# Edge counts from two columns beside the products, and another order of the low halves in two expert networks

## The chip, the cores and the metric

The kernel runs on one core of one Trainium2 chip. The metric is the device time of one execution in microseconds (us). All engines of the core work in parallel and wait for each other with semaphores: TensorE (PE; its weight loads are shown as PEld), VectorE (DVE), ScalarE (ACT), GpSimd (POOL) and the queue of SyncE (SP), which here only starts transfers.

## The reference, cut to what matters

Two graph blocks over 625 nodes of 768 numbers; each ends in a network of eight experts, of which every node takes two.

```python
def _rgcn_conv(x, src, dst, etype, W, root, b):         # twice in block 0
    seg = dst * num_rel + etype                         # 8 relations
    sums = segment_sum(x[src], seg)
    cnt = segment_sum(ones(edges), seg)
    mean = sums / maximum(cnt, 1.0)[:, None]
    out = einsum('nri,rio->no', mean, W)
    return out + x @ root + b

def _L0_ffn_ref(x, ...):            # 8 experts, three products each
    h = gelu(x @ W1[e] + b1[e])     # 768 -> 192
    h = gelu(h @ W2[e] + b2[e])     # 192 -> 384
    y = h @ W3[e] + b3[e]           # 384 -> 768
    out = out + comb[..., e:e+1] * y

def _L1_ffn_ref(x, ...):            # 8 experts, two products each
    h = gelu(x @ w1[e] + b1[e])     # 768 -> 1152
    y = h @ w2[e] + b2[e]           # 1152 -> 768
    out = out + y * gates[:, e:e+1]
```

## The kernel before, in words

Every fp32 matrix is split into a high half (the number rounded to fp32r, names in _hi) and a low half (what is left, names in _lo); a product is then three matmuls (`mm3`: lines 614, 617, 618), or two where one factor is exact. The 625 nodes are five tiles of 128 rows.

**Means of the first relational layer.** For each of the 8 relations r and each half c of 384 columns, the products of all nodes with W[r] are computed first, as rows ("products"). They go to HBM through `stage` and come back one half-relation h = 2r+c at a time (`back_load`, line 739) into one of three places (held0, product0, product1). ACT writes the high half (`part_back_hi`, line 1046), DVE the low half (`part_back_lo`, line 1594). The number of edges between each pair of nodes is an integer matrix `adj`; ACT turns the 5x5 blocks of relation r into `a_rel` (`convert`, line 1053). Then PE, in `means`, sums the products over the sources: for each of the five target tiles t ten matmuls (five source tiles, high and low; line 2395) into one of four banks in turn. At c = 0 five more matmuls with two columns of ones go first (line 2385); they give the edge count of each target row in another bank. DVE takes the count, limits it to 1 from below (line 1600), takes the reciprocal (line 1602), and adds sum times reciprocal to `acc_rows` (line 1618), which frees the bank: PE's tile number m waits until DVE is through with m-4 (`agg_used`). For h+1, DVE's low half stands ahead of the five additions of h.

**Experts.** The rows of the nodes are sorted into 17 slots of 128 rows, each with one expert. Network 0 (n = 0) has three layers, network 1 (n = 1) two. The work is a pipeline of turns: in one turn PE does layer 0 of slot v+1 (or v+2), then layer 1 (and 2) of the slots behind it. The weights of a layer come in units (n = 0: one unit for each layer, of 1152, 768 and 2304 columns; n = 1: three units of 2304 columns for each of the two layers). A unit is loaded by SP into one of four places `weight_raw` (line 780), split by ACT (`high`, line 1108) and DVE (`low`, line 1821) into one of four places of `weight_hi` and `weight_lo`, and used by PE. The load of unit u+4 waits for `low` of u, `high` of u+4 waits until PE has used u. ACT and DVE run four units ahead of PE.

The inputs of a layer are transposed by PE (line 2480): at the start of a turn the inner rows of layers 1 and 2 (`h_rows`, into `hT`), and, after the first unit of layer 0, the rows of the next slot (`slot_in`, into `xt`). ACT and DVE copy them out of the banks as high and low half (lines 1122 and 1831). The banks are few: in network 1 the transposes of `slot_in` use banks 5 and 6, which those of `h_rows` used before, so they wait for DVE's low half of `hT`. DVE copies the last layer's result out (`output`, line 1839); ACT sends it to HBM (`rows_out`, line 1135) and starts the load of a later slot (`rows_in`, line 1114).

Each engine works through its own list in the order in which the code writes it.

## Time and profile before

| | us |
|---|---|
| median of 3 runs | 2444.22 (2434.64 to 2444.30) |
| the profiled execution | 2444.68 |
| its span, first to last instruction | 2442.9 |
| PE busy | 2146.1 (88%) |
| PEld busy | 2054.8 (84%) |
| DVE busy | 1428.3 (58%) |
| ACT busy | 953.6 (39%) |
| POOL busy | 448.8 (18%) |
| means of the first relational layer | 605.2 to 775.0 |
| turns of the experts, n = 0 | about 1265 to 1425 |
| turns of the experts, n = 1 | about 2040 to 2416 |

Times of the profile count from the first instruction. Busy shares are means over stages with different limits. Matmuls are pipelined: one of 384 columns is shown as 0.34 us long and the next begins 0.17 us after it, so their starts tell the pace. A wait is written behind a row in brackets, with the engine and the line that ended it. An issue to the queues (SPq, ACTq) is not busy time.

### The profile page before, as it was taken

The numbers are of one execution on the slowest core, as the hardware profiler recorded it, in microseconds if no ns is written. First come the engines' busy times: TensorE is split into PE (matmuls) and PEld (weight loads), VectorE is DVE, ScalarE is ACT, GpSimd is POOL, SyncE is SP. The second block draws the span as 40 slices with busy tenths as digits, with TensorE's granted clock in tenths as the row PEclk, the third lists the DMA queues.
The fourth block names the chain that finished last, engine by engine and source line by source line (L and its number), as shares of the span: only waits on it lengthen the run. The fifth ranks groups of instructions, "written<-read, shape, count | busy, mean of one in ns | idle before, by whom it ended". The sixth has DMA issues, their size and how long they took to land. (4 is left out here: it accounts for less than half of the span.)

```text
span 2442.9 us, 32630 instructions
## 1 busy us (share of the span) xinstructions
PE 2146.1 (88%) x13045; PEld 2054.8 (84%) x13045; DVE 1428.3 (58%) x2288; ACT 953.6 (39%) x1249; POOL 448.8 (18%) x230
## 2 busy tenths in 40 slices
PE   4898999999999999999968859788878968999994
PEld 4787999998999999999848849677778947999994
DVE  8555455554654133333458774358874677888884
ACT  1333166665332021112126623125522225777672
POOL 4771300000300533443010022211120020000001
PEclk9898999999999999999969979899999978999997
DMA  3412233333322111110259951110122038999995
GB/s 102 137 34 86 72 102 119 111 116 118 116 98 72 58 59 40 41 57 20 62 172 306 313 204 59 46 44 27 61 62 82 1 145 296 347 349 347 358 335 181
DMA packets 158240, 326.96 MB, mean 134 GB/s; under 512 B 14120, under 2 KB 99336, under 8 KB 158090
## 3 DMA queue, kind: packets, MB, share of 16 engines
q1 hardware_dynamic: 133354, 265.68, 31.9%
q10 hardware_dynamic: 18976, 43.33, 4.9%
q0 software_dynamic: 5760, 15.86, 2.1%
q8 instruction: 104, 1.70, 0.3%
q14 instruction: 46, 0.38, 0.0%
HBM read 278.24 MB, written 46.51 MB: 133 GB/s over the span
## 5 line engine op out<-in xcount | busy, mean ns | idle before, releaser
L614 PE MATMUL banks<-weight_hi,xt_hi 128*128 128x384 f32 (+2 forms) x2208 | 740.1, 335 | 69.5 <-DVE xt_lo L1372 14.4
L617 PE MATMUL banks<-weight_lo,xt_hi 128*128 128x384 f32 (+2 forms) x2208 | 723.7, 328 | 0.0
L618 PE MATMUL banks<-weight_hi,xt_lo 128*128 128x384 f32 (+2 forms) x2208 | 723.5, 328 | 0.0
L614 PEld LDWEIGHTS banks<-weight_hi,xt_hi 128*128 128x128 f32 x2208 | 428.5, 194 | 81.9 <-issue 26.4
L617 PEld LDWEIGHTS banks<-weight_lo,xt_hi 128*128 128x128 f32 x2208 | 428.6, 194 | 0.5 <-issue 0.4
L618 PEld LDWEIGHTS banks<-weight_hi,xt_lo 128*128 128x128 f32 x2208 | 427.6, 194 | 0.0
L1821 DVE TENSOR_TENSOR weight_lo<-weight_raw,weight_hi 128x2304 fp32r<-128x2304 f32 (+2 forms) x153 | 342.6, 2243 | 88.8 <-ACT weight_hi L1108 88.7
L1108 ACT ACTIVATE weight_hi<-weight_raw 128x2304 fp32r<-128x2304 f32 (+2 forms) x153 | 287.1, 1880 | 75.7 <-PE banks L614 45.5
L814 POOL TENSOR_TENSOR weight_hi<-weight_raw,zero_col 128x2304 fp32r<-128x2304 f32 (+1 forms) x23 | 95.8, 4164 | 790.9 <-PE banks L614 376.7
L2395 PE MATMUL banks<-held_hi,a_rel 128*128 128x384 f32 x550 | 189.1, 344 | 0.3 <-DVE held_lo L1594 0.3
L2395 PE MATMUL banks<-held_lo,a_rel 128*128 128x384 f32 x550 | 187.6, 341 | 0.0
L614 PE MATMUL banks<-weight_hi,hT_hi 128*128 128x384 f32 (+1 forms) x442 | 151.6, 343 | 25.5 <-DVE hT_lo L1831 25.5
L1588 DVE TENSOR_TENSOR held_lo<-banks,held_hi 128x384 fp32r<-128x384 f32 x80 | 44.6, 557 | 209.3 <-ACT held_hi L1041 209.3
L617 PE MATMUL banks<-weight_lo,hT_hi 128*128 128x384 f32 (+1 forms) x442 | 150.2, 340 | 0.0
L618 PE MATMUL banks<-weight_hi,hT_lo 128*128 128x384 f32 (+1 forms) x442 | 149.9, 339 | 0.0
L1041 ACT ACTIVATE held_hi<-banks 128x384 fp32r<-128x384 f32 x80 | 39.2, 490 | 242.0 <-PE banks L618 242.0
L1576 DVE TENSOR_TENSOR adj<-adj,banks 128x640 f32 x80 | 65.4, 818 | 116.2 <-PE banks L2367 116.2
L911 POOL TENSOR_TENSOR weight_lo<-weight_raw,weight_hi 128x1536 fp32r<-128x1536 f32 (+2 forms) x16 | 70.0, 4373 | 320.1 <-ACT weight_hi L987 320.1
L1053 ACT ACTIVATE a_rel<-adj 128x640 fp32r<-128x640 uint16 x80 | 58.2, 743 | 174.7 <-PE banks L2395 174.7
L816 POOL TENSOR_TENSOR weight_lo<-weight_raw,weight_hi 128x2304 fp32r<-128x2304 f32 (+1 forms) x23 | 124.5, 5412 | 1.8
L614 PEld LDWEIGHTS banks<-weight_hi,hT_hi 128*128 128x128 f32 (+1 forms) x442 | 83.7, 189 | 29.6 <-DVE weight_lo L1821 21.7
L2395 PEld LDWEIGHTS banks<-held_hi,a_rel 128*128 128x128 f32 x550 | 105.3, 191 | 0.4 <-DVE held_lo L1594 0.4
(397 smaller groups left out, 3722.9 us busy)
## 6 DMA issues: line engine op xcount, KB each, us to landing
weight_raw<-L_ffn_w_in SPq DMA_DIRECT2D x102, 1152.0 KB, 6.4
weight_raw<-L_gnn_W_in SPq DMA_DIRECT2D x32, 1152.0 KB
weight_raw<-L_ffn_W_in SPq DMA_DIRECT2D x17, 1152.0 KB, 7.5
products<-bias_rows SPq DMA_DIRECT2D x80, 192.0 KB, 1.9
slot_in<-slot_rows ACTq DMA_DIRECT2D x34, 384.0 KB, 6.3
slot_out<-bias_rows ACTq DMA_DIRECT2D x34, 384.0 KB, 6.1
weight_raw<-L_ffn_W_in SPq DMA_DIRECT2D x17, 576.0 KB, 6.8
product_back<-products SPq DMA_DIRECT2D x10, 960.0 KB, 4.8
```

What stands on the lines that cost most here:

```text
L614: ins = pe.matmul(dst, s[0], m[0], start=start, stop=False)
L617: pe.matmul(dst, s[0], m[1], start=False, stop=False)
L618: return pe.matmul(dst, s[1], m[0], start=False, stop=stop)
L814: pool.tensor_tensor(hi, raw[s][0:rows, 0:n], zero_col[0:rows, :].broadcast_to([rows, n]), ALU.add).then_inc(hi_ready, 1)
L816: pool.tensor_tensor(lo, raw[s][0:rows, 0:n], f32(hi), ALU.subtract).then_inc(unit_ready, 1)
L911: pool.tensor_tensor(lo, raw[u.slot][:, 0:n], f32(hi), ALU.subtract).then_inc(unit_ready, 1)
L1053: act.activation(A_r[:, t, :, :], adj[:, r * TILES:(r + 1) * TILES, t * P:(t + 1) * P], ACT.Copy).then_inc(a_ready, 1)
L1108: act.activation(W4[u % RING][0][0:rows, 0:k * cols], RAW4[u % RAWS][0:rows, 0:k * cols], ACT.Copy).then_inc(e_hi[n], 1)
L1576: vec.tensor_tensor(block_of, block_of, ps[:, 2 * (s % 2):2 * (s % 2) + 2, 0:HALF], ALU.add).then_inc(slot_done, 1)
L1588: vec.tensor_tensor(lo[:, t, :], ps[:, part_bank(1, n), 0:WCOL], f32(hi[:, t, :]), ALU.subtract).then_inc(part_lo, 1)
L1821: vec.tensor_tensor(lo, RAW4[u % RAWS][0:rows, 0:k * cols], f32(hi), ALU.subtract).then_inc(e_lo[n], 1)
L2395: ins = pe.matmul(ps[:, agg_bank(m), 0:WCOL], A_r[:, t, src, :], part[:, src, :], start=(src == 0 and i == 0), stop=(src == FULL and i == 1))
```

## The change

1. **Counts.** The five matmuls with two columns of ones are gone, and with them the semaphore `cnt_full` and PE's wait for `cnt_ready`. The high halves of the three places have 386 columns instead of 384; ACT writes ones into the last two once for each place (`part_back_hi`, h < 3). At c = 0 the matmul with the high half is 386 columns wide, so that the count stands in column 384 of the same bank as the sums. For the last source tile the low half goes first, so that the wide matmul ends the bank. DVE takes the count from there, once all ten matmuls are done. In the second relational layer held0 keeps the row step of 386.
2. **Experts, DVE.** In each turn the low halves of `hT` and the output of the turn before go ahead of the last `low` of the turn before.
3. **Experts, n = 1.** The transposes of the next slot, their high and low halves and `rows_in` come after the second unit of layer 0 (`NEXT_AFTER`) and no longer after the first.
4. **Experts, ACT.** `rows_out` goes behind layer 0's part of the turn.
5. Small tensors are put together to make room for the 128 bytes `product_end`; the other tensors move by 64 or 128 bytes.

```diff
+OCOL = WCOL + 2
@@ places: the high halves of held0, product0 and product1 are [P, TILES, OCOL]
+        NEXT_AFTER = [0, 1]
@@ part_back_hi (ACT)
                 act.wait_ge(part_in[h % BACKS], 16 * (h // BACKS + 1))
-                act.activation(places[0][h % BACKS][0][:, :, :], back_rows[h % BACKS][:, :, :], ACT.Copy).then_inc(part_hi, 1)
+                hi = places[0][h % BACKS][0]
+                if h < BACKS:
+                    act.activation(hi[:, :, WCOL:OCOL], f32(ones_r[:, 0:TILES * (OCOL - WCOL)]).rearrange("p (t n) -> p t n", t=TILES), ACT.Copy)
+                act.activation(hi[:, :, 0:WCOL], back_rows[h % BACKS][:, :, :], ACT.Copy).then_inc(part_hi, 1)
@@ experts (ACT)
-                    if turn > 0:
-                        rows_out(turn - 1)
-                    for l, v in visits(n, turn):
+                    for i, (l, v) in enumerate(visits(n, turn)):
                         for j in range(parts(n, l)):
...
-                            if l == 0 and j == 0 and v + 1 < XSLOTS:
+                            if l == 0 and j == NEXT_AFTER[n] and v + 1 < XSLOTS:
                                 transposed_hi(0, v + 1)
                                 rows_in(v + 3)
                             high()
+                        if i == 0 and turn > 0:
+                            rows_out(turn - 1)
@@ inverse (DVE)
-                vec.wait_ge(cnt_full, r * TILES + t + 1)
-                order.step(vec.tensor_scalar(cnt_m[:, one], ps[:, (r * TILES + t) % 4, 0:1], 1.0, None, ALU.max))
+                m = agg_number(0, r, 0, t)
+                vec.wait_ge(agg_full, m + 1)
+                order.step(vec.tensor_scalar(cnt_m[:, one], ps[:, agg_bank(m), WCOL:WCOL + 1], 1.0, None, ALU.max))
@@ experts (DVE)
                         if l > 0:
                             transposed_lo(l, v)
+                    if turn > 0:
+                        output(turn - 1)
+                    if turn > turns(n)[0]:
+                        low()
+                    lows_left = sum(parts(n, l) for l, _ in visits(n, turn)) - 1
                     for l, v in visits(n, turn):
                         for j in range(parts(n, l)):
-                            if l == last and j == parts(n, l) - 1:
-                                output(v)
-                            if l == 0 and j == 0 and v + 1 < XSLOTS:
+                            if l == 0 and j == NEXT_AFTER[n] and v + 1 < XSLOTS:
                                 transposed_lo(0, v + 1)
-                            low()
+                            if lows_left > 0:
+                                low()
+                                lows_left -= 1
+                output(XSLOTS - 1)
@@ means (PE)
-                        if layer == 0 and c == 0:
-                            q = r * TILES + t
-                            if q >= 4:
-                                pe.wait_ge(cnt_ready, q - 3)
-                            for src in range(TILES):
-                                ins = pe.matmul(ps[:, q % 4, 0:2], A_r[:, t, src, :], ones_r[:, 0:2], start=(src == 0), stop=(src == FULL))
-                            ins.then_inc(cnt_full, 1)
...
+                        wide_cols = OCOL if layer == 0 and c == 0 else WCOL
                         for src in range(TILES):
-                            for i, part in enumerate(places[layer][(2 * r + c) % len(places[layer])]):
+                            for part, cols in ((hi, wide_cols), (lo, WCOL)) if src < FULL else ((lo, WCOL), (hi, wide_cols)):
@@ layer, in the experts (PE)
-                        if l == 0 and j == 0 and v + 1 < XSLOTS:
+                        if l == 0 and j == NEXT_AFTER[n] and v + 1 < XSLOTS:
                             transposes_of(0, v + 1)
```

DVE in a turn of the second experts before, from the fifth `low` of a turn on (rows with x5 are five instructions):

```order
L1821 TENSOR_TENSOR weight_lo<-weight_raw,weight_hi 128x2304 x5
L1839 COPY bias_rows<-banks 128x384 x2
L1821 TENSOR_TENSOR weight_lo<-weight_raw,weight_hi 128x2304
L1831 TENSOR_TENSOR hT_lo<-banks,hT_hi 128x384 x3
L1831 TENSOR_TENSOR xt_lo<-banks,xt_hi 128x3x128 x2
```

And after the change, the same stretch:

```order
L1829 TENSOR_TENSOR weight_lo<-weight_raw,weight_hi 128x2304 x4
L1839 TENSOR_TENSOR hT_lo<-banks,hT_hi 128x384 x3
L1847 COPY bias_rows<-banks 128x384 x2
L1829 TENSOR_TENSOR weight_lo<-weight_raw,weight_hi 128x2304 x2
L1839 TENSOR_TENSOR xt_lo<-banks,xt_hi 128x3x128 x2
```

The three instructions on `hT` moved ahead of the two copies and of one split of weights; those on `xt` have two splits ahead of them and four behind.

DVE in a turn of the first experts before:

```order
L1821 TENSOR_TENSOR weight_lo<-weight_raw,weight_hi 128x2304
L1839 COPY bias_rows<-banks 128x384 x2
L1821 TENSOR_TENSOR weight_lo<-weight_raw,weight_hi 128x1152
L1831 TENSOR_TENSOR hT_lo<-banks,hT_hi 96x256
L1831 TENSOR_TENSOR hT_lo<-banks,hT_hi 128x384
L1831 TENSOR_TENSOR xt_lo<-banks,xt_hi 128x3x128 x2
L1821 TENSOR_TENSOR weight_lo<-weight_raw,weight_hi 96x768
```

And after:

```order
L1829 TENSOR_TENSOR weight_lo<-weight_raw,weight_hi 128x2304
L1839 TENSOR_TENSOR hT_lo<-banks,hT_hi 96x256
L1839 TENSOR_TENSOR hT_lo<-banks,hT_hi 128x384
L1847 COPY bias_rows<-banks 128x384 x2
L1829 TENSOR_TENSOR weight_lo<-weight_raw,weight_hi 128x1152
L1839 TENSOR_TENSOR xt_lo<-banks,xt_hi 128x3x128 x2
L1829 TENSOR_TENSOR weight_lo<-weight_raw,weight_hi 96x768
```

Here too `hT` goes ahead of the copies and of the unit of 1152 columns.

PE in the means, the end of one target tile at c = 0 and the start of the next, before:

```order
L2395 MATMUL banks<-product_hi,a_rel 128x384
L2395 MATMUL banks<-product_lo,a_rel 128x384
L2385 MATMUL banks<-ones_r,a_rel 128x2 x5
L2395 MATMUL banks<-product_hi,a_rel 128x384
L2395 MATMUL banks<-product_lo,a_rel 128x384
```

And after:

```order
L2405 MATMUL banks<-product_hi,a_rel 128x386
L2405 MATMUL banks<-product_lo,a_rel 128x384 x2
L2405 MATMUL banks<-product_hi,a_rel 128x386 x2
L2405 MATMUL banks<-product_lo,a_rel 128x384
L2405 MATMUL banks<-product_hi,a_rel 128x386
```

The five short matmuls are gone, and the order of high and low is turned round at the last source tile.

## Rows read from the trace of the kernel before

**Rows 1.** The page: busy tenths of PE and of DMA in 40 slices.

```profile
PE   4898999999999999999968859788878968999994
DMA  3412233333322111110259951110122038999995
```

**Rows 2.** Windows: from:to, length, busy (xcount) of PE, PEld, DVE, ACT, POOL; clock; DMA share, GB/s.

```profile
633.77:774.82 141.05, 141.05 (x876) 140.91 (x875) 78.19 (x153) 45.66 (x44) 0.00 (x0) 1.00 0.29 101
605.20:619.00 13.80, 13.48 (x49) 13.42 (x49) 3.89 (x2) 6.01 (x6) 9.99 (x3) 0.51 0.80 306
```

**Rows 3.** Timeline of PEld in the means: start, length, instruction, count, idle before.

```profile
642.77 0.70 PEld L2385 LDWEIGHTS banks<-ones_r,a_rel 128*128 128x128 f32 x5
...
643.50 0.19 PEld L2395 LDWEIGHTS banks<-product_lo,a_rel 128*128 128x128 f32 x1
643.68 0.19 PEld L2395 LDWEIGHTS banks<-product_hi,a_rel 128*128 128x128 f32 x1
```

**Rows 4.** All instructions of line 2385: count, duration min/median/max in ns.

```profile
L2385 PE MATMUL banks<-ones_r,a_rel x200: 165/250/352, 605.2 to 764.2; 128*128 128x2 f32 x100
```

**Rows 5.** Timeline of PE and DVE in the first relation.

```profile
606.72 0.69 PE L2395 MATMUL banks<-held_hi,a_rel 128*128 128x384 f32 x1 [0.28 <-DVE held_lo L1594]
...
616.57 3.61 DVE L1594 TENSOR_TENSOR product_lo<-product_back,product_hi 128x1920 fp32r<-128x1920 f32 x1 [9.91 <-ACT product_hi L1046]
...
621.46 0.42 PE L2395 MATMUL banks<-held_hi,a_rel 128*128 128x384 f32 x1
...
631.92 0.45 PE L2395 MATMUL banks<-product_hi,a_rel 128*128 128x384 f32 x1 [1.53 <-DVE acc_rows L1618]
```

**Rows 6.** Timeline of DVE at the start of a later relation.

```profile
656.64 2.16 DVE L1594 TENSOR_TENSOR product_lo<-product_back,product_hi 128x1920 fp32r<-128x1920 f32 x1 [1.79 <-ACT product_hi L1046]
658.71 0.15 DVE L1600 TENSOR_SCALAR cnt_m<-banks 128x1 f32<-128x1 f32 x1
...
659.10 0.62 DVE L1618 SCALAR_TENSOR_TENSOR acc_rows<-banks,inv,acc_rows 128x384 f32<-128x384 f32 x1
```

**Rows 7.** Who waited for whom in 2030 to 2443: total, times, longest.

```profile
PE banks L2480 <- DVE hT_lo L1831: 17.1, 14, 1.3
```

**Rows 8.** Timeline of PE, DVE and ACT in two turns of the second experts.

```profile
2205.13 0.92 PE L2480 MATMUL banks<-ident,slot_in 128*128 128x128 f32 x6 [1.19 <-DVE hT_lo L1831]
...
2221.62 1.14 PE L2480 MATMUL banks<-ident,h_rows 128*128 128x128 f32 x9
...
2223.57 1.01 DVE L1839 COPY bias_rows<-banks 128x384 f32<-128x384 f32 x2
...
2226.97 1.48 DVE L1831 TENSOR_TENSOR hT_lo<-banks,hT_hi 128x384 fp32r<-128x384 f32 x3
...
2224.02 0.85 ACT L1122 ACTIVATE hT_hi<-banks 128x384 fp32r<-128x384 f32 x2
...
2238.23 2.14 ACT L1108 ACTIVATE weight_hi<-weight_raw 128x2304 fp32r<-128x2304 f32 x1 [0.85 <-PE banks L614]
```

**Rows 9.** Windows of the experts: one turn and 15 us (n = 1); 15 us and 13 turns (n = 0).

```profile
2201.14:2223.57 22.43, 21.24 (x128) 20.82 (x127) 18.50 (x13) 15.86 (x15) 0.00 (x0) 1.00 0.96 347
2105.00:2120.00 15.00, 13.81 (x85) 13.39 (x84) 12.27 (x12) 9.33 (x10) 0.00 (x0) 1.00 1.01 380
1345.00:1360.00 15.00, 13.81 (x103) 13.48 (x101) 11.50 (x14) 10.14 (x14) 0.00 (x0) 1.00 1.02 315
1285.87:1405.00 119.13, 102.73 (x718) 99.16 (x716) 95.69 (x119) 79.49 (x118) 0.00 (x0) 1.00 0.97 310
```

**Rows 10.** DMA issues of the page: count, KB each, median us to landing (n = 1, n = 0).

```profile
weight_raw<-L_ffn_w_in SPq DMA_DIRECT2D x102, 1152.0 KB, 6.4
weight_raw<-L_ffn_W_in SPq DMA_DIRECT2D x17, 1152.0 KB, 7.5
```

**Rows 11.** Who waited for whom in 1275 to 1410 (n = 0).

```profile
PE banks L614 <- DVE hT_lo L1831: 18.3, 15, 1.7
ACT weight_hi L1108 <- DMA weight_raw<-L_ffn_W_in: 6.8, 4, 2.4
```

More of the change, by code:

```diff
@@ L38 @@
 WCOL = 384
+OCOL = WCOL + 2
+PRODUCT_END = 32
 UNIT = KD * WCOL
@@ L158, in build @@
             one, pair = allocator(here)
-            back_pairs = [pair(f"product{k}", [P, TILES, WCOL]) for k in range(2)]
+            back_pairs = [(one(f"product{k}_hi", [P, TILES, OCOL], F32R), one(f"product{k}_lo", [P, TILES, WCOL], F32R)) for k in range(2)]
         with ExitStack() as here:
@@ L254, in build @@
             one, _ = allocator(here)
-            one("held0_hi_place", [P, TILES, WCOL], F32)
+            one("held0_hi_place", [P, TILES, OCOL], F32)
             back_rows.insert(0, one("held0_back", [P, TILES, WCOL], F32))
-        held = [rg2("held0", [P, TILES, WCOL])]
+        held = [(rg("held0_hi", [P, TILES, OCOL], F32R), rg("held0_lo", [P, TILES, WCOL], F32R))]
         with ExitStack() as here:
@@ L2392, in means @@
                             pe.wait_ge(agg_used, m - 3)
+                        hi, lo = places[layer][(2 * r + c) % len(places[layer])]
+                        wide_cols = OCOL if layer == 0 and c == 0 else WCOL
                         for src in range(TILES):
-                            for i, part in enumerate(places[layer][(2 * r + c) % len(places[layer])]):
-                                ins = pe.matmul(ps[:, agg_bank(m), 0:WCOL], A_r[:, t, src, :], part[:, src, :],
-                                                start=(src == 0 and i == 0), stop=(src == FULL and i == 1))
-                                if unit_done and c == 0 and t == 0 and src == 0 and i == 0:
+                            for part, cols in ((hi, wide_cols), (lo, WCOL)) if src < FULL else ((lo, WCOL), (hi, wide_cols)):
+                                begin, end = src == 0 and part is hi, src == FULL and part is hi
+                                ins = pe.matmul(ps[:, agg_bank(m), 0:cols], A_r[:, t, src, :], part[:, src, 0:cols], start=begin, stop=end)
+                                if unit_done and c == 0 and t == 0 and begin:
                                     ins.then_inc(unit_used, 1)
```

24 lines of the change are left out of this document (11 added, 13 removed).

## The prediction, made blind

> **What bounds the kernel now.** I read the busy tenths of the page first: PE is near full almost everywhere, and DMA is near full in two places, the turns of the first experts (slices 21 to 23) and of the second (slices 34 to 39) [rows 1]. A change on PE's list outside these two counts in full; inside them it counts only as far as the transfers can follow. Then I read the stages that the diff touches. In the means PE has no gap from 633.77 on: 141.05 us busy in 141.05 us, at the full clock (1.00, 2.4 GHz), DMA at 0.29, DVE busy 78.19 [rows 2]. PE alone is the bound there. In a turn of the second experts PE works 21.24 of 22.43 us [rows 9] and the rest is one gap of 1.19 us, the transposes of `slot_in` waiting for `hT_lo` [rows 8]; it comes 14 times, 17.1 us [rows 7]. In the first experts PE works 102.73 of 119.13 us in 13 turns, 7.90 of 9.16 us for each [rows 9]; there the first matmul of layer 1 waits for the same kind of instruction, 15 times, 18.3 us in all [rows 11].
>
> **Counts.** Five short matmuls make the next tile late. Weight loads of matmuls with 384 columns start 0.174 us apart. With a group of five from 642.77 on, the second load behind it starts at 643.50 and the next at 643.68 [rows 3]; without the group they would be the second and third load from 642.77, at 642.94 and 643.12. So one group costs 0.56 us. There are 200 such matmuls, 40 groups [rows 4], 35 of them after 633.77. A sum that proves the price: seven relations are 700 matmuls of 0.1735, 121.5 us, and 35 groups of 0.56, 19.6 us; together 141.1 against the 141.05 measured [rows 2]. All 35 groups are on the path, since PE never waits there: 19.6 us.
>
> The other five groups are in the first relation, and I count nothing for them. PE starts it at 606.72, when the low half of held0 is there [rows 5], at half the clock (0.51, 1.2 GHz, until 619.00; PE had stood 2.4 us before) [rows 2], and ACT's new instruction, 10 columns wide, goes ahead of it and may cost 0.2. The fifth tile begins at 621.46 now. It needs the first bank, which DVE can't free before its low half of product0 is done, at 616.57 + 3.61 = 620.18, plus count, reciprocal and addition, about 1.0: 621.2. So the tile starts at most 0.3 earlier. Then DVE's next low half, slow beside POOL, holds PE until 631.92 (1.53 us) [rows 5]; PE that comes earlier only waits longer.
>
> The wide matmul streams 386 columns instead of 384. By the pace of 0.174 us for 384 that is 0.9 ns more, 200 times, 0.2 us. No row shows a row step of 386 or this width. The other end: two columns by themselves take 0.56/5 = 0.11 us, 22 us in all, which would eat the gain. Below nothing I exclude, since no column is saved. I take 0.2, as the columns follow one another in one stream, and keep the other end as a rival.
>
> DVE now takes the count after the ten matmuls. From the count to the addition are 0.39 us (658.71 to 659.10) and the addition takes 0.62 [rows 6]. That is 1.0 us for a tile, and PE needs the bank three tiles (5.2 us) later, so it is hidden, except where DVE comes late anyway: at the start of a relation the low half of the next product stands ahead. The relation of rows 6 starts on PE at 653.97, DVE frees its first bank at 659.72, 5.75 us later; PE's fifth tile will start after 4 x 1.735 = 6.94 us. A margin of 1.2 us is left, of 4.0 before. The list of ACT and the loads from HBM follow the same matmuls and move with them.
>
> **Second experts.** Set the start of a turn, 2221.62, to 0. Now DVE does two copies (from 1.95) and one `low` (2.5 us) and only then `hT_lo`, 5.35 to 6.8 [rows 8]. After the change `hT_lo` comes first. It waits for ACT's `hT_hi`, whose first part is there at about 2.9, and ends at about 4.5, 2.3 us earlier. The transposes that waited for it also move behind the second unit, to about 7.8. Both together leave over 3 us of margin; the gap goes. What is next on PE is its own work, 21.24 us for a turn.
>
> The postponed `low` ends 2.5 us later, and the load behind it starts later. It lands 6.4 us after its issue [rows 10]: 2226.97 + 2.5 + 6.4 = 2235.9. ACT needs it at 2238.23, or 1.2 earlier in a shorter turn, 2237.0 [rows 8]. So 1.1 us is left of what was 4.9. PE needs the unit some 4 us after ACT and DVE have split it, which covers a small delay.
>
> The limit is what all transfers can do. A turn of 22.43 us has a DMA share of 0.96, 21.5 us of full use, 347 GB/s. The best 15 us show a share of 1.01 and 380 GB/s [rows 9]. So a turn can't be shorter than 21.5/1.01 = 21.3 us, by chance PE's own 21.24. I take 1.0 us of the 1.19, as both are then full and no delay is made good: 14 turns, 14 us. The ends are 0 (transfers already give all) and 17.1.
>
> The Trainium skill, page "DMA: Bandwidth & Descriptors", section "Where 436 GB/s comes from", says that for transfers between HBM and SBUF about 358 GB/s of HBM is the limit. The 380 GB/s over 15 us speak against it on this core. By the rule a turn would take 347 x 22.43 / 358 = 21.7 us and the gain of this part would be 10 us instead of 14.
>
> **First experts.** Here `hT_lo` goes ahead of two copies (1.0 us) and a `low` of 1152 columns, and the gap of 1.2 us would go. But 13 turns have a share of 0.97 (8.9 us of 9.16), and the best 15 us have 1.02, at 315 GB/s [rows 9]: a turn can't be shorter than 8.9/1.02 = 8.7 us. ACT already waits for loads four times, 6.8 us [rows 11], and a large unit lands only after 7.5 us [rows 10]. I take 0.4 us for each of 15 turns, 6 us; the ends are 0 and 18.3. `rows_out` now stands behind layer 0; its buffer is written again two turns later, so it costs nothing, and ACT is free earlier for `h_rows`.
>
> **What it costs.** In the last turn of each network there is no layer 0 to cover the copies of slot 15: DVE does them after `hT_lo` now and PE waits for the first of the two, 0.5 us, twice: 1 us. `rows_in` and the three extra instructions of ACT are off the path.
>
> **The sum.** 2444.68 - 19.6 + 0.2 - 14 - 6 + 1 = 2406.3; the profiled execution was within 0.5 us of the median, 2444.22. One of the three runs was 10 us faster, which I can't explain. Forecast: 2406 us, its own range 2399 to 2413.
>
> **The rivals.**
> A, transfers are full in both experts: the gaps only change their name, from `hT_lo` to the loads. For it: shares of 0.96 and 0.97, and the waits for loads. Against it: 380 GB/s over 15 us. Then the counts gain 19.4 and the experts 3: 2444.7 - 22 = 2422. The page's limit of 358 GB/s is a weak form of it (2410, inside my own range). Chance 0.17.
> B, transfers hinder nowhere: both gaps go whole, 17.1 + 18.3 + 19.4 - 1 = 54: 2391. Against it speaks the best share in the first experts. Chance 0.12.
> C, DVE's chain in the means is late: the margin of 1.2 us is too small, say by 2 us in each of seven relations, 14 us: 2420. For it: the low half waits for ACT at each relation's start. Chance 0.07.
> D, 386 columns don't stream at the old pace: the gain of the counts is lost, 2425. Chance 0.04.
> E, slower: the postponed `low` starves the loads. They would have to land over 3 us later than the 6.4 and 7.5 us now, since ring and split cover that much. To lose the 19.4 us of the counts, all of some 30 turns must become 0.65 us longer than today. With 1.3 us for each: 2444.7 - 19.4 + 39 = 2464. Chance 0.02.
> The forecast has 0.55; 0.03 is left for mixtures.
>
> **Range and chances.** 2396 to 2423 takes in the forecast, A and C and a part of the mixtures, 0.8. A measurement of this kernel can tell about 0.5% (12 us) from no change. Faster by more: the forecast, A, B, C and most of D, 0.94; within 0.5%: 0.04; slower: 0.02.
>
> **What would show it.** In the means no row with two columns, PE full, and the stretch of seven relations 121.7 us long instead of 141.05. The fifth tile of each relation must not wait for the addition (C), and the matmuls with 386 columns must start 0.174 us apart (D). In the second experts: no wait of the transposes for `hT_lo`, the copies of line 1847 about 21.4 us apart, DMA share near 1. In the first: 8.7 us apart. Waits of ACT's `weight_hi` for loads instead would mean A, turns of 7.9 us B. I would be wrong most easily in the size of what the transfers allow.

## The result, and the profile after

The changed kernel takes **2411.47 us** (median of 4 runs, 2405.89 to 2420.97), the kernel before 2443.45 us beside it: a ratio of **0.9886, 95% interval 0.9862 to 0.9910**, some 28 us (22 to 34) less. The forecast was 2406 us, 2396 to 2423.

The busy tenths of PE and DMA on the page after, which answer to [rows 1]. No slice differs from before by more than one tenth: at this grain the page doesn't show the change.

```profile
PE   4898999999899999999969849788888868999994
DMA  3412223332432111110159951110122027999995
```

Windows of after (from:to, length, busy and count of PE, PEld, DVE, ACT, POOL; clock; DMA share, GB/s): 135 us of the means, 12 turns of the second experts, 14 turns of the first. They answer to [rows 2, 9].

```profile
629.00:764.00 135.00, 135.00 (x758) 134.82 (x757) 88.81 (x166) 48.63 (x48) 6.99 (x2) 0.98 0.32 113
2103.01:2359.54 256.53, 255.22 (x1520) 252.21 (x1519) 219.83 (x157) 187.95 (x169) 0.00 (x0) 1.00 0.97 365
1276.87:1398.90 122.03, 107.62 (x747) 104.17 (x746) 103.94 (x126) 85.90 (x123) 0.00 (x0) 1.00 0.91 309
```

PE has no gap in the means, and none to speak of in the second experts (21.38 us for a turn, was 22.43). In the first experts a turn takes 8.72 us (was 9.16), and PE still idles 14.4 us of 122. Who waits there now (total us, times, longest), from 1265 to 1410 us, and ACT alone in the second experts, from 1968 to 2391 us:

```profile
ACT weight_hi L1115 <- DMA weight_raw<-L_ffn_W_in: 28.0, 26, 2.4
...
PE banks L618 <- DVE hT_lo L1839: 14.3, 10, 4.4
PEld banks L618 <- DVE weight_lo L1829: 13.2, 8, 4.7
```

```profile
ACT weight_hi L1115 <- DMA weight_raw<-L_ffn_w_in: 74.0, 48, 4.3
```

Before, ACT waited 6.8 us for loads in the first experts [rows 11], and in the second the list of its waits from 2030 us on has none for a load. The 17.1 us of [rows 7] are gone.

Next I cut both profiles at the same matmuls. These are windows of before and, below them, of after: the relations' products, the means, layer 2, the first experts, the part between, the second experts.

```profile
309.27:606.72 297.45, 294.74 (x1749) 273.05 (x1748) 150.00 (x324) 194.45 (x251) 0.00 (x0) 1.00 0.34 111
606.72:776.23 169.51, 166.75 (x995) 166.11 (x996) 95.85 (x177) 53.11 (x52) 20.23 (x4) 0.96 0.32 112
776.23:1211.79 435.56, 426.06 (x2450) 425.22 (x2451) 141.25 (x209) 72.49 (x132) 158.28 (x45) 0.99 0.13 41
1211.79:1442.23 230.44, 169.59 (x1039) 153.97 (x1040) 163.84 (x268) 118.40 (x172) 22.96 (x19) 0.86 0.79 259
1442.23:1917.89 475.66, 388.96 (x2597) 371.50 (x2598) 298.83 (x663) 146.49 (x261) 70.92 (x17) 0.92 0.17 57
1917.89:2415.10 497.21, 444.07 (x2582) 426.25 (x2580) 387.38 (x416) 284.78 (x269) 13.89 (x23) 0.94 0.75 277
```

```profile
314.44:613.66 299.22, 295.12 (x1743) 273.33 (x1743) 150.11 (x324) 194.77 (x252) 0.00 (x0) 1.00 0.33 110
613.66:765.37 151.71, 144.84 (x800) 144.22 (x800) 95.72 (x177) 53.24 (x54) 20.18 (x4) 0.97 0.35 125
765.37:1204.64 439.27, 429.77 (x2450) 428.92 (x2451) 141.34 (x209) 72.70 (x132) 158.36 (x45) 1.00 0.13 41
1204.64:1428.88 224.24, 168.48 (x1039) 153.74 (x1040) 164.57 (x268) 119.23 (x172) 22.95 (x19) 0.86 0.78 265
1428.88:1908.41 479.53, 395.75 (x2597) 378.30 (x2598) 298.88 (x663) 146.66 (x261) 72.06 (x18) 0.90 0.17 56
1908.41:2391.53 483.12, 443.99 (x2582) 428.88 (x2580) 383.36 (x416) 281.05 (x269) 13.89 (x23) 0.94 0.76 285
```

The three stages that the diff touches give 17.8 + 6.2 + 14.1 = 38.1 us, almost what I had summed (38.4, with 1 us for the ends taken off). But the spans differ by only 23.7 us. 5 us are start-up: the first matmuls with `rf` start at 34.3 to 34.9 us in some executions and at 39.6 to 40.2 in others, whatever the kernel. The rest stands in rows that nobody looks at after such a change: **layer 2 has the same 2450 matmuls and the same 9.5 us in which PE is idle, and takes 3.7 us more**; the relations' products take 1.8 more, the part between 3.9. That was the open question.

One thing ahead: executions of one kernel differ by up to 20 us here (before: 2425 to 2451 over all runs). The profiles show where: 5 us at the start, and up to 12 us between 104 and 241 us, in the first mixer (124.8 to 137.2 us, whatever the kernel). No part of the change is there. I didn't look for its cause. So I compare stages of profiles for what is under 10 us, and ratios of many runs for the rest.

### The profile page after: what moved, and what is told of

It reads as the page before. It is cut to its first block and busy times, and to the rows that moved or that the text cites. A ratio compares the mean times of both kernels' runs of the same rounds, so it can differ in the third digit from the quotient of the medians.

```text
span 2419.2 us, 32227 instructions
## 1 busy us (share of the span) xinstructions
PE 2134.1 (88%) x12845; PEld 2045.4 (85%) x12845; DVE 1429.5 (59%) x2288; ACT 951.5 (39%) x1252; POOL 450.8 (19%) x230
## 5 line engine op out<-in xcount | busy, mean ns | idle before, releaser
L818 POOL TENSOR_TENSOR weight_hi<-weight_raw,columns 128x2304 fp32r<-128x2304 f32 (+1 forms) x23 | 95.7, 4160 | 784.0 <-PE banks L618 360.9
L2405 PE MATMUL banks<-held_hi,a_rel 128*128 128x384 f32 (+1 forms) x550 | 172.5, 342 | 9.7 <-DVE acc_rows L1626 5.6
L2405 PE MATMUL banks<-held_lo,a_rel 128*128 128x384 f32 x550 | 169.3, 340 | 0.0
L621 PE MATMUL banks<-weight_lo,hT_hi 128*128 128x384 f32 (+1 forms) x442 | 151.2, 342 | 0.0
L622 PE MATMUL banks<-weight_hi,hT_lo 128*128 128x384 f32 (+1 forms) x442 | 150.9, 341 | 0.0
```

Of the source, the lines that this page charges most:

```text
L621: pe.matmul(dst, s[0], m[1], start=False, stop=False)
L622: return pe.matmul(dst, s[1], m[0], start=False, stop=stop)
L818: pool.tensor_tensor(hi, raw[s][0:rows, 0:n], zero_col[0:rows, :].broadcast_to([rows, n]), ALU.add).then_inc(hi_ready, 1)
L2405: ins = pe.matmul(ps[:, agg_bank(m), 0:cols], A_r[:, t, src, :], part[:, src, 0:cols], start=begin, stop=end)
```

## Experiments

**1. Each part by itself, and the two halves of the experts' part.** `counts_only` has the counts' part alone, `experts_only` the experts' part alone. `move_only` and `order_only` are counts_only with one more edit each. move_only moves the transposes of `slot_in`:

```
         NEXT_AFTER = [0, 1]
...
-                            if l == 0 and j == 0 and v + 1 < XSLOTS:
+                            if l == 0 and j == NEXT_AFTER[n] and v + 1 < XSLOTS:
```

order_only is the changed kernel with `NEXT_AFTER = [0, 0]`: VectorE's and ScalarE's new order, transposes at the old place.

> The counts alone (two columns of ones, 386 columns), both experts in the old order. My theory: the 35 groups of 0.56 us were wholly on PE's path, so 19.4 us go, 0.992 of the time before (2424 of 2443 us), and the means from the first held_hi matmul to the transposes behind them take about 151.7 us instead of 169.5, as in the changed kernel's profile. Rival: the first relation gives a part back (there PE now waits 5.6 us for DVE's additions, where it waited 1.5), so that only some 13 to 15 us go, 0.994. In the experts nothing changes: turns of 22.4 us (second) and 9.16 us (first).

> The experts' edits alone, the counts as before. My theory: 14.9 us in the second experts and 6 us in the first, less 1 at the ends: about 20 us, 0.992 of the time before; turns of 21.4 us and 8.7 us. Rival (the transfers take it back): the measured ratio of the whole change, 0.9886, is only 28 us where the two stages and the means together should give 38, so the experts would give only some 8 to 10 us outside the one profiled execution, 0.996.

> The counts, and of the experts' edits only the place of the transposes of slot_in: behind the second unit in the second experts (NEXT_AFTER), with VectorE's old order (copies and a low half ahead of hT_lo). Theory: each of the two edits closes the gap of 1.19 us by itself, since PE comes to the transposes some 4 us later than now while hT_lo is as early as before. So the second experts give the whole 15 us, turns of 21.4 us, and nothing comes of the first: 2443 - 19.4 - 15 = 2409, 0.986. Rival: the place alone does not do, because hT_lo then holds something later (layer 1's matmuls), and turns stay above 22 us: 2420 or more.

> The counts, and of the experts' edits VectorE's new order (hT_lo ahead of copies and low half) with the copy of rows behind layer 0, but the transposes of slot_in stay behind the first unit (NEXT_AFTER = [0, 0]). Theory: hT_lo ends 2.3 us earlier, its first part at about 3.4 us of a turn where PE comes at 4.7, so the gap closes without the move: 2443 - 19.4 - 15 - 5 = 2404, 0.984, the same time as the whole change within 0.2%. Rival: hT_hi of ACT or the postponed low half holds PE in the place of the gap, turns of 22 us, 2412 or more.

Measured against before, on one chip: counts_only 0.9978 [0.9958, 0.9997], experts_only 0.9908 [0.9885, 0.9932], move_only 0.9875 [0.9854, 0.9897], order_only 0.9883 [0.9856, 0.9911].

So the experts give 22 us, as much as I had thought and not less. The **counts give only some 5 us**, although their own stage shrinks from 169.5 to 151.6 us in the profile, nearly as predicted. Neither of my two theories has that: the loss isn't in the first relation either. And move_only and order_only both come out where the whole change does: each closes the gap of 1.19 us by itself.

The profile of counts_only has the long layer 2 as well, and that of experts_only hasn't. The windows of layer 2 in experts_only and counts_only (order_only has 439.27 us too):

```profile
772.64:1208.32 435.68, 426.17 (x2450) 425.32 (x2451) 141.44 (x209) 72.72 (x132) 158.31 (x45) 0.99 0.13 41
```

```profile
749.80:1189.18 439.38, 429.89 (x2450) 429.03 (x2451) 141.33 (x209) 72.59 (x132) 158.33 (x45) 1.00 0.13 41
```

It follows the counts' part, not the execution. The weight loads of PE in this stage, one after the other, before and after (start, length):

```profile
819.94 0.19 PEld L614 LDWEIGHTS banks<-weight_hi,xt_hi 128*128 128x128 f32 x1
...
821.33 0.19 PEld L618 LDWEIGHTS banks<-weight_hi,xt_lo 128*128 128x128 f32 x1
```

```profile
819.84 0.19 PEld L621 LDWEIGHTS banks<-weight_lo,xt_hi 128*128 128x128 f32 x1
...
821.25 0.19 PEld L618 LDWEIGHTS banks<-weight_hi,xt_hi 128*128 128x128 f32 x1
```

Eight steps take 1.39 us before (0.174 each) and 1.41 after (0.176). The means of the starts of matmuls with 384 columns, one after the other, tell the two levels apart: 173.8 ns in layer 2 before, 175.9 after; 174.9 against 176.0 in the relations' products. The clock granted over layer 2 is 0.99 before and 1.00 after, so it is not what makes after the longer. Apart from the row step that `held0_hi` keeps in layer 2, these stages have no instruction that the counts' part changed. What they share with it is where things lie: the wider `product_hi` pushed the weights up by 128 bytes of each partition, `weight0_hi` from byte 81024 to 81152, `weight0_lo`, `weight1_hi` and `weight1_lo` by as much. Their addresses left 128 when divided by 512 before, and leave 256 now.

**2. Addresses alone.** `layout_before` is the kernel before with the weights at the changed kernel's addresses; `weight_raw`, `ident` and `ones_r` move up by the same 128 bytes, some small tensors are packed together, and no operation is another. `after_res128` and `after_res384` are the changed kernel with 384 or 128 bytes of small tensors put ahead of the weights:

```
         keep("product_end", [P, PRODUCT_END], F32)
+        stats = keep("stats", [P, TILES, 2, 6], F32)
+        norms = keep("norms", [P, 6 * TILES], F32)
         raw = [keep(f"weight_raw{s}", [P, UNIT], F32) for s in range(2)]
...
-        stats = keep("stats", [P, TILES, 2, 6], F32)
-        norms = keep("norms", [P, 6 * TILES], F32)
```

> The kernel before with nothing changed but addresses: the small tensors packed together and a filler of 128 bytes, so that weights and raw weights lie 128 bytes higher, exactly where the changed kernel has them (weight0_hi at byte 81152 of a partition instead of 81024). Theory (layout): in all four profiles of kernels with the counts' part, matmuls with 384 columns start 175.5 to 176.2 ns apart, even in stages whose instructions the change does not touch, against 173.4 to 175.0 in the two kernels without it; the addresses of the weights are the only thing that these stages share. Then this kernel's matmuls take 176 ns between 300 and 600 and 775 and 1200 us, the stretch from the end of the means to the first experts takes 439.3 us instead of 435.6, and the whole is 8 to 10 us slower than before, 1.004. Rival: something else of the counts' part does it (or chance), and this kernel shows 173.4 to 175.0 and 1.000.

> The changed kernel with stats and norms (384 bytes) allocated ahead of the weights, so that all weights again lie at the remainder by 512 that they had before (128), nothing else. Layout theory: matmuls start 173.4 to 175.0 ns apart again, the stretch from means to first experts takes 435.6 us, and the whole gains 8 to 10 us on the changed kernel: 0.985 of before. Rival: no difference, 0.9886 and 176 ns.

> The changed kernel with norms (128 bytes) alone ahead of the weights: their addresses leave 384 by 512, and 128 by 256. If the pace goes by the remainder by 256, it is the fast one, 173.4 to 175.0 ns, 0.985; if by 512 or more, it stays at about 176 ns, 0.9886.

Measured: layout_before **1.0052 [1.0029, 1.0074]**, after_res128 **0.9857 [0.9834, 0.9880]**, after_res384 0.9867 [0.9840, 0.9893]. Layer 2 in these three:

```profile
773.43:1214.49 441.06, 431.56 (x2450) 430.71 (x2451) 141.33 (x209) 72.62 (x132) 158.20 (x45) 0.99 0.13 41
```

```profile
752.91:1189.89 436.98, 427.48 (x2450) 426.63 (x2451) 141.39 (x209) 72.60 (x132) 158.23 (x45) 0.99 0.13 41
```

```profile
752.97:1189.96 436.99, 427.50 (x2450) 426.64 (x2451) 141.32 (x209) 72.61 (x132) 158.23 (x45) 0.99 0.13 41
```

The kernel before becomes 0.5% slower (12.7 us, 7 to 18) by addresses alone. In its layer 2 the matmuls on the weights start 176.0 ns apart, as in after, where before has 173.4. In after_res128 and after_res384 they are back at 173.4. By the ratios after_res128 gains some 7 us on the changed kernel, but the two intervals overlap: the pace shows the gain, the time by itself does not. Remainders of 128 and 384 do the same, 256 is slow: this speaks for the remainder by 256.

I had expected 439.3 us for layer 2 of layout_before and 435.6 for that of after_res128; both are longer, 441.1 and 437.0. Two other things move this stage. The first is the clock. PE stands for 3.03 us at its start, waiting for `xt_lo`, and what follows differs, here before and after:

```profile
782.75 0.69 PE L614 MATMUL banks<-weight_hi,xt_hi 128*128 128x384 f32 x1 [3.03 <-DVE xt_lo L1372]
```

```profile
771.90 0.45 PE L618 MATMUL banks<-weight_hi,xt_hi 128*128 128x384 f32 x1 [3.03 <-DVE xt_lo L1379]
```

In counts_only, after, move_only, order_only and after_res288 PE goes on at the full clock; in the other nine profiles 7 to 17 matmuls behind the wait start 0.32 us apart, at half the clock (1.2 GHz). The first 20 us of layer 2 in before, after, layout_before, after_res128 and first_relation (experiment 4):

```profile
776.23:796.23 20.00, 16.97 (x99) 16.74 (x100) 8.14 (x17) 7.03 (x15) 0.00 (x0) 0.91 0.00 1
765.37:785.37 20.00, 16.97 (x107) 16.73 (x108) 8.67 (x18) 7.05 (x15) 0.00 (x0) 1.00 0.00 1
773.43:793.43 20.00, 16.97 (x91) 16.73 (x92) 8.14 (x17) 7.04 (x15) 0.00 (x0) 0.83 0.00 1
752.91:772.91 20.00, 16.97 (x99) 16.74 (x100) 8.14 (x17) 7.04 (x15) 0.00 (x0) 0.91 0.00 1
749.36:769.36 20.00, 16.97 (x92) 16.74 (x93) 8.13 (x17) 7.04 (x15) 0.00 (x0) 0.83 0.00 1
```

In the same 16.97 busy us PE does 107 matmuls in after and 91 in layout_before. The late starts add up to 1.3, 0.1, 2.5, 1.6 and 2.4 us; without them layer 2 takes 434.3, 439.2, 438.6, 435.3 and 435.6 us. So the weights' place costs layer 2 4.3 us in the kernel before and 3.8 in the changed one, more than the bare windows say.

The second is `held0` and `held1`, whose 800 matmuls belong to layer 2. They start 174.7 ns apart in before, layout_before and experts_only and 175.9 to 176.3 in every kernel with the counts' part, wherever the weights lie: 1.0 us, the rest between 434.3 and 435.3. There `held0_hi` has rows of 1544 bytes and the three other halves lie 64 bytes higher; no run takes these two apart.

**3. What the counts' part is worth, and one more address.** `counts_res128` is counts_only with the same 384 bytes ahead of the weights. `after_res288` is the changed kernel with only `columns` (32 bytes) ahead of them.

> The counts' part alone (both experts in the old order), with the 384 bytes of stats and norms ahead of the weights, so that the weights lie at the old remainder by 512 (128). The same part at the new addresses gave a ratio of only 0.9978 [0.9958, 0.9997], some 5 us. Theory: the part itself is worth nearly the 19.4 us that I predicted (17.8 us in the means by the profile), and the addresses took 8 to 10 of them in stages that it does not touch: 2438 - 18 = 2420, 0.9925. Rival: the part is worth 5 to 10 us wherever the weights lie, 0.996 to 0.998.

> The changed kernel with the weights only 32 bytes higher (remainder 288 by 512, 32 by 256). Slow was 256 (changed kernel, layout_before), fast were 128 and 384. If only a start at a multiple of 256 is slow, this one is fast: the stretch from the means to the first experts 437.0 us, 0.986. If it is a start at 128 by 256 that is fast, this one is slow: 439 us or more, 0.989 or above.

Measured: counts_res128 **0.9923 [0.9898, 0.9948]**, 18.7 us (13 to 25). The rival is out: by itself the part is worth what the sum said. The two ratios differ by 13 us (6 to 21), which the addresses had taken. The pace of the matmuls with 384 columns accounts for some 8 of them: 1.4 us in the products, 4.0 in layer 2, 1.7 between the experts, 1.2 in the second experts. after_res288 0.9828 [0.9797, 0.9860], its layer 2:

```profile
744.63:1181.22 436.59, 427.09 (x2451) 426.24 (x2451) 141.28 (x209) 72.62 (x132) 158.36 (x45) 1.00 0.13 41
```

So for these weights 32 bytes past a multiple of 256 is faster than a start at a multiple of 256. This window has none of the half-clock starts; by pace the order in layer 2 is 173.4 ns at 128 or 384, 174.0 at 288 and 176.0 at 256. In the relations' products it is another: 173.9 ns at 288, 174.9 at 128 or 384, 176.0 at 256.

This is no rule for every operand. `held0` and `held1` begin at multiples of 256 in before (bytes 179712 to 202752) and run at 174.7 ns, faster than with three of their halves 64 bytes past it. The other operand of the weights' matmuls, `xt`, lay at byte 31872 in all kernels, 128 past a multiple of 256; whether the distance to it counts was not tested. The rows show the pace by address, not what in the chip makes it.

**4. The first relation.** In after PE waits 5.64 us for VectorE's additions at the fifth tile of the first relation. The timeline of PE, DVE, ACT and GpSimd there:

```profile
628.01 0.66 PE L2405 MATMUL banks<-held_hi,a_rel 128*128 128x386 f32 x1 [5.64 <-DVE acc_rows L1626]
```

```profile
623.05 3.90 DVE L1601 TENSOR_TENSOR product_lo<-product_back,product_hi 128x1920 fp32r<-128x1920 f32 x1 [9.54 <-ACT product_hi L1053]
...
632.53 5.55 DVE L1601 TENSOR_TENSOR product_lo<-product_back,product_hi 128x1920 fp32r<-128x1920 f32 x1
```

```profile
621.11 0.21 ACT L1052 ACTIVATE product_hi<-ones_r 128x10 fp32r<-128x10 f32 x1 [6.66 <-DMA product_back<-products]
```

```profile
615.72 4.03 POOL L818 TENSOR_TENSOR weight_hi<-weight_raw,columns 128x2304 fp32r<-128x2304 f32 x1 [322.98 <-DMA weight_raw<-L_gnn_root_in]
619.83 5.11 POOL L820 TENSOR_TENSOR weight_lo<-weight_raw,weight_hi 128x2304 fp32r<-128x2304 f32 x1
```

`product_back` lands late: two root loads of 1152 KB stand ahead of it in SyncE's queue, and the low halves take 3.90 and 5.55 us beside GpSimd, where others take 2.16. `first_relation` is after_res128 with the root loads behind `back_load(2)` and GpSimd's split behind VectorE's third low half:

```
-            pair_load(U_ROOT2, "L0_gnn_root2")
...
                 back_load(h)
+                if h == 2:
+                    pair_load(U_ROOT2, "L0_gnn_root2")
...
             pool.wait_ge(unit_ready, U_ROOT2)
+            pool.wait_ge(part_lo, 3)
```

> after_res128 and in addition the first relation of the means relieved: the two root loads of 1152 KB are issued behind the first two loads of product_back, and GpSimd splits them only when VectorE has made three low halves. In the changed kernel's profile PE waits 5.64 us at the fifth tile there for VectorE's additions, behind a low half that came late (product_back landed at about 621) and took 3.90 us beside GpSimd, where others take 2.16. Theory: the wait shrinks to under 1 us, the means take 5 us less (about 146 from the first held_hi matmul to the transposes behind them, less what the pace gives), 0.983 of before. Rival: the low halves of the second relation take 3.6 us beside GpSimd instead and use up the margin of 1.2 us at its fifth tile, so that the wait only moves there and less than 2 us are gained.

The ratio is 0.9846 [0.9819, 0.9874], which doesn't tell it from after_res128. The means do (after_res128 ahead, then first_relation):

```profile
601.77:752.91 151.14, 145.08 (x800) 144.43 (x800) 95.41 (x177) 53.24 (x54) 20.20 (x4) 0.96 0.35 125
```

```profile
603.09:749.36 146.27, 143.33 (x801) 142.40 (x801) 96.31 (x177) 53.30 (x54) 20.28 (x4) 0.98 0.37 132
```

```profile
607.65 2.16 DVE L1603 TENSOR_TENSOR product_lo<-product_back,product_hi 128x1920 fp32r<-128x1920 f32 x1 [4.71 <-ACT product_hi L1055]
...
633.65 6.65 DVE L1603 TENSOR_TENSOR product_lo<-product_back,product_hi 128x1920 fp32r<-128x1920 f32 x1
```

```profile
640.88 0.44 PE L2407 MATMUL banks<-held_hi,a_rel 128*128 128x384 f32 x1 [1.66 <-DVE acc_rows L1628]
```

The means gain 4.9 us, as expected, but in two steps. In the first relation the low half takes 2.16 us again and PE no longer waits at the fifth tile: the relation takes 19.9 us and no longer 27.0. In the second relation the low halves now stand beside GpSimd, 3.48 and 6.65 us long, and PE waits 1.66 us: the other seven take 2.2 us more. So the rival is there, in a small form. Which of the two edits did how much was not told apart. Layer 2 takes 1.1 us longer (438.1 against 437.0); 0.8 of it are its 16 half-clock starts, where after_res128 has 10.

**5. Transfers, and the best pieces together.** `light_loads` is the changed kernel with half (or a third) of each unit loaded from the 25th on, so it leaves out over half of the expert weights:

```
+                    kk = k // 2 if u >= 24 and k > 1 else k
...
-                    sp.dma_start(RAW4[s][0:rows, 0:k * cols].rearrange("p (k n) -> p k n", k=k),
+                    sp.dma_start(RAW4[s][0:rows, 0:kk * cols].rearrange("p (k n) -> p k n", k=kk),
```

> The changed kernel, but from the 25th unit of each expert network on only the first half (or third) of a unit's rows is loaded, so over half of the expert weights are left out. It shows whether the loads still hold the turns. My theory in the prediction (transfers full in both): in the first experts turns fall from 8.72 us to PE's own 7.9 us, some 10 us for the stage; in the second, where PE is busy 255.2 of 256.5 us already, only 0.1 us for a turn is left and ScalarE's 74 us of waits for loads go without the time moving. Rival for the first experts: VectorE's or ScalarE's chain holds them, turns stay above 8.4 us.

The turns of the first experts can be read at the transposes of `h_rows`, in after and in light_loads:

```profile
1322.91 0.71 PE L2489 MATMUL banks<-ident,h_rows 128*96 128x128 f32 x5
1332.07 0.71 PE L2489 MATMUL banks<-ident,h_rows 128*96 128x128 f32 x5
1340.79 0.71 PE L2489 MATMUL banks<-ident,h_rows 128*96 128x128 f32 x5
```

```profile
1333.12 0.71 PE L2490 MATMUL banks<-ident,h_rows 128*96 128x128 f32 x5
1340.79 0.71 PE L2490 MATMUL banks<-ident,h_rows 128*96 128x128 f32 x5
1348.46 0.71 PE L2490 MATMUL banks<-ident,h_rows 128*96 128x128 f32 x5
```

It was run once, for its profile (2384.22 us). With light loads seven turns in a row take 7.64 to 7.71 us; in after the same seven take 8.0 to 10.5, mean 9.0. So **in the first experts the loads hold the turns**, and the rival of VectorE's chain is out. The stage takes 215.6 us, 8.6 less. In the second experts nine of fourteen turns of after take 21.03 to 21.08 us and five are longer (21.15 to 22.57), and light_loads has 21.03 to 21.08 in all; the stage takes 6.4 us less, and ScalarE's waits for loads go from 74.0 to 6.0 us. I had expected 0.1 for a turn: the loads still cost single turns there, and the end. From the last transposes of `h_rows` to the last matmul there are 15.4 us before, 17.8 in after, 14.8 in light_loads.

`combined` is first_relation with VectorE's and ScalarE's new order in the first experts only, and the moved transposes in the second:

```
-                    if turn > 0:
+                    if n == 0 and turn > 0:
                         output(turn - 1)
-                    if turn > turns(n)[0]:
+                    if n == 0 and turn > turns(n)[0]:
                         low()
...
+                            if n == 1 and l == last and j == parts(n, l) - 1:
+                                output(v)
```

> The best pieces together: the first_relation kernel (counts, weights at remainder 128, root loads and GpSimd's split later), and in the second experts VectorE's and ScalarE's old order beside the moved transposes, the new order only in the first experts. In the profiles of the changed kernel and of after_res128, ScalarE waits 72 to 74 us for loads in the second experts and the stage takes 480.4 to 482.8 us; with one of the two edits alone it waits 0 (move only) and 10 us (order only), and the stage takes 478.5 and 479.2. Theory: both together close the same gap twice and only postpone the loads; with the move alone there the stage takes 478.5 us, the means 146.3: 3 us less than first_relation, 0.983 of before. Rival: the difference of 2 to 4 us between these profiles is chance, and the time is first_relation's, 0.9846.

Measured **0.9798 [0.9773, 0.9822]**, 2382.70 us (before 2433.44 on that chip): the lowest ratio of all, and faster than the changed kernel, whose interval (0.9862 to 0.9910) lies wholly above. The interval of after_res288 (0.9797 to 0.9860) overlaps its own. Its means take 146.4 us, its second experts 476.5 us, every turn 21.01 us, 15.4 us at the end. It keeps PE without a gap over 200 us:

```profile
2050.00:2250.00 200.00, 200.00 (x1201) 199.33 (x1200) 175.96 (x125) 150.39 (x135) 0.00 (x0) 1.00 1.00 376
```

The ratio is better than the 0.983 that I gave; the stages account for first_relation's time less 5 us, and the rest, some 7 us, lies within the two intervals. ScalarE still waits 34.9 us for loads in its second experts, where move_only had no such wait; I take it that at the faster pace of PE the loads have less time; no run shows it. That "both edits together only postpone the loads" agrees with the stage lengths below, 479.5 to 482.8 us in the six profiles with both edits and all loads against 476.5 to 479.2 in the three with one, but each kernel was profiled only once, and the margin is 0.3 us.

The stages of all profiles (us; cut at the same matmuls as above, the second experts up to the start of the last matmul):

| kernel | products | means | layer 2 | experts 1 | between | experts 2 |
|---|---|---|---|---|---|---|
| before | 297.5 | 169.5 | 435.6 | 230.4 | 475.7 | 496.9 |
| layout_before | 298.5 | 169.5 | 441.1 | 227.5 | 478.7 | 499.5 |
| counts_only | 299.2 | 151.6 | 439.4 | 227.3 | 476.8 | 497.5 |
| counts_res128 | 297.6 | 151.2 | 436.8 | 231.4 | 473.4 | 496.9 |
| experts_only | 297.5 | 169.5 | 435.7 | 227.0 | 476.4 | 479.6 |
| after | 299.2 | 151.7 | 439.3 | 224.2 | 479.5 | 482.8 |
| move_only | 299.2 | 152.2 | 439.2 | 227.3 | 477.2 | 478.5 |
| order_only | 299.2 | 151.8 | 439.3 | 225.5 | 478.4 | 479.2 |
| after_res128 | 297.6 | 151.1 | 437.0 | 223.0 | 476.4 | 481.7 |
| after_res384 | 297.6 | 151.0 | 437.0 | 222.6 | 475.0 | 480.4 |
| after_res288 | 296.6 | 151.7 | 436.6 | 225.3 | 471.9 | 479.5 |
| first_relation | 297.6 | 146.3 | 438.1 | 226.7 | 474.9 | 481.2 |
| combined | 297.6 | 146.4 | 438.1 | 226.7 | 472.7 | 476.5 |
| light_loads | 299.2 | 150.9 | 440.7 | 215.6 | 475.2 | 476.4 |

## Why the prediction was right, and where it wasn't

**Counts, 19.6 us: right in size and place.** The means went from 169.5 to 151.7 us, 17.8 less. The missing 1.8 are the pace again: from the second relation on the matmuls of the means start 175.4 ns apart, where the sum had 173.5, and over 700 of them that is 1.3 us. Here too rows and places differ: the high halves have rows of 1544 bytes, the low halves and `product1_hi` lie 64 or 128 bytes higher. No run takes these apart; after_res128 has the same 175.4. Counting nothing for the first relation was right too, it takes 27.5 us before and after: PE waits 5.64 us where it waited 1.53 [rows 5], as "PE that comes earlier only waits longer" said, though by more than I had seen.

**The wide matmul, 0.2 us: nearly.** The ends were 0.2 and 22. From the second relation on, matmuls on `held0` start 175.4 ns apart in the halves where all are narrow and 177.3 where every other one is wide; on `product0` and `product1` it is 174.8 and 175.1. That is 3.8 ns for a wide matmul in the one place and 0.5 in the others instead of 0.9, 0.3 to 0.4 us in all. Rival D is out. Rival C, VectorE too late for the fifth tile, is out: PE is busy 135.00 of 135.00 us behind the first relation.

**The step that failed** is one that I didn't write: that what the diff doesn't touch stays as it is. The part on tensors and their places moved the weights onto a multiple of 256 bytes, and the matmuls with them as moving operand start up to 1.5% later one after the other. The windows grow by 1.8 us in the relations' products and 3.7 in layer 2; with the half-clock starts taken off, layer 2 grows by 4.9, of which 1.0 is `held0` and `held1`. By the ratio of layout_before the addresses cost 12.7 us (7 to 18), by the pace of all stages some 8, by after against after_res128 some 7. The sum had no term for it. It can be the greater part of what the measured time (28 us less, 22 to 34) lacks of the forecast (38); the time still lay in the range because the range had been made wide for another reason, rival A. The diff showed the new addresses; I read its part on `columns`, `norms` and `product_end` as book-keeping.

**Second experts, 14 us: right sum, wrong terms.** The stage gave 14.1 us. I had taken 1.0 of 1.19 us for a turn, with a floor of 21.3 us that transfers set and 21.24 that PE's own work sets. Both floors were too high: undisturbed turns take 21.03 us, 1.45 less than the 22.48 before. PE's 21.24 busy us in a turn with a gap held 0.26 us that go with the gap. The matmul ahead of it counts with its 0.34 us instead of the 0.17 until the next could start, and the six transposes behind it start over 0.68 us instead of 0.57 (their row is 0.92 us long in [rows 8], and 0.82 where there is no gap, as in experts_only):

```profile
2213.14 0.82 PE L2489 MATMUL banks<-ident,slot_in 128*128 128x128 f32 x6
```

And the transfers do 375 GB/s over 200 us (move_only) where I had only 15 us of 380 to go by:

```profile
2050.00:2250.00 200.00, 200.00 (x1198) 199.34 (x1198) 176.23 (x126) 149.79 (x138) 0.00 (x0) 1.00 1.01 375
```

That could have given 20 us. Loads that come late in single turns and at the end took some 6 of them back, as light_loads shows. The mechanism that I had feared in a small way (rival E, the postponed `low` starves the loads) is real but small, and unneeded: move_only and order_only close the gap alone and their stages take 478.5 and 479.2 us.

The Trainium skill, page "HBM Reference", section "Specifications (TRN2)", says that a core streaming alone gets well above its share of about 358 GB/s. The 375 GB/s agree with it. By that page the 358 GB/s are each core's share when both cores of a domain stream; the section that I weighed in the prediction gives the limit without this condition.

**First experts, 6 us: the size was luck.** The pair of profiles gives 6.2. But the stage varies by 4 us between profiles of kernels with the same order there: the five profiles in VectorE's old order have 227.3 to 231.4, mean 228.8, the eight full-load ones in the new order 222.6 to 227.0, mean 225.1. So the order gives some 3.7 us. The reason was right: turns of 7.67 us, PE's own, take turns with ones of 9 to 14 us in which a load is missing, and only fewer bytes change that. This is rival A, in this one stage.

**The ends, +1 us: too small.** 2.4 us for the second experts alone (15.4 to 17.8), and by the loads, not by the copies: ACT waits for them up to the last unit.

```profile
2369.02 2.13 ACT L1115 ACTIVATE weight_hi<-weight_raw 128x2304 fp32r<-128x2304 f32 x1 [2.20 <-DMA weight_raw<-L_ffn_w_in]
```

## What to carry to other kernels

A diff that widens a tensor moves every tensor behind it. Compare the addresses of the matmuls' operands before and after, and look at the pace of matmuls in stages that the change does not touch: the same matmuls in a longer window at the same clock are a finding, not noise. But look at the granted clock of the stage's first microseconds too before a difference of 1 or 2 us is explained. When two edits each close the same gap, try each alone, and look first at the one that doesn't postpone loads. And when a transfer limit is to be the floor of a sum, read it from the longest stretch there is, since busy time of an engine that still has gaps is no floor for it either.

## What I had not expected of the hardware

- The start-to-start time of matmuls with 384 columns of 4 bytes differs with the place of their operands. With the weights as moving operand and `xt` at one place, rows that start at a multiple of 256 bytes give 176.0 ns, 128 past it 173.4 (layer 2) and 174.9 (products), 32 past it 174.0 (layer 2) and 173.9 (products), all at a granted clock of 1.00. With `held0`, `held1` and `a_rel` a multiple of 256 is not slow: 174.7 ns.
- Behind the same wait of 3.03 us the same matmuls run at the full clock in five profiles of fourteen and start at half of it in nine, for 7 to 17 matmuls, up to 2.5 us.
- VectorE's subtraction over 128x1920 takes 2.16 us alone and 3.48 to 6.65 beside GpSimd's splits.
- One core's loads run at 375 GB/s for 200 us in which PE is busy for 200.00.

What stays open: what makes the pace go by address, why 32 bytes past is faster than 128 in the products and slower in layer 2, why layout_before has 175.6 ns in the products where after has 176.0 with the weights at the same place, how the clock behind the wait is decided, what the part between the experts varies by (471.9 to 479.5 us, with a granted clock of 0.92 in before and 0.90 in after), and the 12 us of the first mixer. Combined with the weights at 288 was not run.
